# Three more groups of the shared expert behind the last routing step, five instead of eight in the last stage, four outgoing buffers there

## The reference: what is computed

```python
b, s, d = x.shape
T = b * s
xf = x.reshape(T, d)
shared = jax.nn.silu(xf @ Sg) * (xf @ Su) @ Sd          # Sg, Su: 256 x 256, Sd: 256 x 256
probs = jax.nn.softmax(xf @ Wr, axis=-1)                 # 16 experts
topk_p, topk_i = jax.lax.top_k(probs, K)                 # K = 2
...
    y = jax.nn.silu(xf @ wg) * (xf @ wu) @ wd
    return (acc + y * c[:, None], None)
...
return (routed + shared).reshape(b, s, d)
...
x = x + _L1_ffn_ref(_layernorm(x, axis=-1), L1_ffn_Wr, L1_ffn_Wg, L1_ffn_Wu, L1_ffn_Wd, L1_ffn_Sg, L1_ffn_Su, L1_ffn_Sd)
```

## Time and profile before

| | us |
|---|---|
| median of three runs | 1645.22 |
| the profiled execution | 1644.97 |
| its span | 1643.2 |
| PE busy in it | 1487.4 (91%) |
| DVE busy in it | 1018.6 (62%) |
| last instruction of VectorE in `finish` ends | 1640.5 |

### The profile page before, as it was taken

The page is one execution under the profiler, slowest core; times in us unless marked ns, Lnnn a source line. Parts: engine busy times, 40 slices in busy tenths (PEclk is TensorE's granted clock), DMA queues, the critical chain, the costliest instruction groups (busy, mean ns, idle before and its releaser), DMA issues. The chain is left out here.

```text
span 1643.2 us, 31228 instructions
## 1 busy us (share of the span) xinstructions
PE 1487.4 (91%) x9905; PEld 1114.3 (68%) x9905; DVE 1018.6 (62%) x3468; ACT 736.6 (45%) x1544; POOL 572.3 (35%) x994
## 2 busy tenths in 40 slices
PE   5999999983999999699799999999999597589987
PEld 3776676772999999565566666666666386468876
DVE  3345555453444444499898888888886286645558
ACT  3444444430222222345177777777777242244420
POOL 4123333344222222245532332322333165635530
PEclk9999999986999999899899999999999798889999
DMA  7001111115777777668857666667761575745556
GB/s 234 1 26 36 49 46 52 39 58 157 212 212 213 212 212 212 211 229 259 203 75 98 98 90 90 92 89 98 98 89 40 143 240 187 171 129 156 161 159 220
DMA packets 150592, 221.74 MB, mean 135 GB/s; under 512 B 23648, under 2 KB 98144, under 8 KB 150304
## 3 DMA queue, kind: packets, MB, share of 16 engines
q1 hardware_dynamic: 127904, 170.58, 45.2%
q0 software_dynamic: 13344, 36.55, 6.4%
q10 hardware_dynamic: 9184, 12.61, 2.5%
HBM read 141.16 MB, written 78.25 MB: 134 GB/s over the span
## 5 line engine op out<-in xcount | busy, mean ns | idle before, releaser
L2095 ACT ACTIVATE t_probs<-t_ps_st 128x512 f32<-128x512 f32 x576 | 313.2, 597 | 124.9 <-PE t_ps_st L2147 122.4
L2073 DVE CUSTOM_DVE_ANT_0 whole_sum<-t_ps_s,t_later 128x512 bf16<-128x512 f32 (+3 forms) x512 | 285.5, 586 | 14.0 <-PE t_ps_s L2133 11.9
L2049 POOL TENSOR_SCALAR_AFFINE_SELECT t_probs<-t_probs 128x128 f32<-128x128 f32 x512 | 137.4, 300 | 330.5 <-ACT t_probs L2095 328.9
L2133 PE MATMUL t_ps_s<-t_ks,t_qs 96*128 96x512 f32 (+3 forms) x768 | 247.8, 362 | 0.5 <-ACT t_neg_max L2085 0.5
L2147 PE MATMUL t_ps_st<-t_qs,t_ks 128*128 128x512 f32 (+3 forms) x768 | 242.7, 365 | 0.8 <-ACT t_probs L2095 0.8
L2147 PEld LDWEIGHTS t_ps_st<-t_qs,t_ks 128*128 128x128 f32 x768 | 136.8, 189 | 73.6 <-ACT t_probs L2095 40.2
L2073 DVE CUSTOM_DVE_ANT_0 whole_sum<-t_ps_s,t_later,t_first_max 128x512 bf16<-128x512 f32 (+3 forms) x256 | 140.5, 549 | 47.8 <-PE t_ps_s L2133 47.8
L2162 PE MATMUL t_ps_o<-t_probs,t_vs 128*17 128x256 f32 (+1 forms) x2560 | 154.9, 361 | 0.5 <-ACT whole_sum L2102 0.5
L2133 PEld LDWEIGHTS t_ps_s<-t_ks,t_qs 96*128 96x128 f32 x768 | 138.7, 190 | 18.0 <-DVE t_first_max L2073 1.6
L1460 POOL DMA_INDIRECT outputs_dram<-m_y,m_place x71 | 68.1, 959 | 208.8 <-DVE m_place L1535 201.1
L1490 PE MATMUL m_ps_h<-m_xt,m_w_t 128*128 128x128 f32 x1136 | 140.7, 278 | 0.0
(11 more groups left out here) (340 smaller groups left out, 2652.1 us busy)
## 6 DMA issues: line engine op xcount, KB each, us to landing
m_w_t<-in_w_dram SPq DMA_DIRECT2D x71, 512.0 KB, 4.4
t_qs<-qkt_dram SPq DMA_DIRECT2D x128, 128.0 KB, 5.6
t_ks<-qkt_dram SPq DMA_DIRECT2D x128, 128.0 KB, 5.7
m_x_t<-gathered_dram SPq DMA_DIRECT2D x79, 128.5 KB, 2.1
m_x_t<-gathered_dram SPq DMA_DIRECT2D x71, 129.0 KB, 2.1
d_ye<-outputs_dram SPq DMA_DIRECT2D x8, 1024.0 KB, 8.2
qkt_dram<-d_hi ACTq DMA_DIRECT2D x32, 256.0 KB, 5.2
qkt_dram<-d_lo SPq DMA_DIRECT2D x32, 256.0 KB, 7.2
```

Of the source, the lines that this page charges most:

```text
L2049: nc.gpsimd.affine_select(out=diag, in_=diag, compare_op=ALU.is_ge, fill=0.0, base=0, pattern=[[1, P]], channel_multiplier=-1).then_inc(ma ...
L2073: nc.vector.tensor_tensor_reduce(out=seen[:, (NP * p + x) % (RS + 1), 0:keys], in0=bank_of(p, x)[:, 0:keys], in1=masks, scale=1.0, scalar= ...
L2095: nc.scalar.activation(probs[:, p % 2, i // NST, base:base + STC], ps_st[(NX * p + i) % RT][:], ACT.Exp, scale=HD ** -0.5).then_inc(exp_re ...
L2133: nc.tensor.matmul(bank_of(p, x)[:, 0:keys], q[0:MAX_ROW, head, qc * P:(qc + 1) * P], k[0:MAX_ROW, head, k0:k0 + keys], start=True, stop=T ...
```

## The change

`finish` now computes the shared expert of five groups (11 to 15), and `back` that of eleven. The three added ones, groups 8 to 10, don't stand in the pipeline of ticks, which stays as it is, but behind it: on TensorE after the last ranking, on VectorE around the making of the tile list, on ScalarE between the closing writes. They use `k_scaled` in place of `k_sh`, and `k_ps_wo` for the result in place of `k_ps_u`, so that one group's way down does not hold up the next one's way up. ScalarE's two exponentials and its last four closing writes move behind added sigmoids.

In `finish` the 16 groups stand in six slots: one gate, then one or two plain groups, then one shared group. `f_y` has four buffers (Y = 4), the wait for a store stands right before the instruction that writes `f_y`, and the stores are issued by ScalarE, behind the sigmoid of the slot; SyncE issues loads alone.

```diff
-SHARED_BACK = 8
+SHARED_BACK = 11
+EARLY_SHARED = 8
...
+            def late_gate(k):
+                dve.wait_ge(sig_ready, k + 1)
+                nc.vector.tensor_tensor(scaled[:, k % 2], ps_g[:], scaled[:, k % 2], ALU.mult).then_inc(gated, 1)
+                dve.wait_ge(gated, k + 1)
+                dve.wait_ge(u_done, k + 1)
+                nc.vector.tensor_tensor(scaled[:, k % 2], ps_u[:], scaled[:, k % 2], ALU.mult).then_inc(h_ready, 1)
+
+            def late_add(k):
+                dve.wait_ge(y_done, k + 1)
+                these = total[:, k * G:(k + 1) * G]
+                nc.vector.tensor_tensor(these, these, ps_wo[k % 2][:], ALU.add).then_inc(y_added, 1)
...
+            for k in range(EARLY_SHARED, SHARED_BACK):
+                late_sigmoid(k)
+                if k - EARLY_SHARED < 2:
+                    close_regions(act, closed[k - EARLY_SHARED], closed[k - EARLY_SHARED + 1])
             act.wait_ge(shifted_ready, 2)
             nc.scalar.activation(soft[:], soft[:], ACT.Exp).then_inc(exp_ready, 1)
             nc.scalar.activation(soft_best[:], soft_best[:], ACT.Exp).then_inc(exp_ready, 1)
-            close_regions(act, E // 2, E)
...
+            def late_up(k):
+                cols = slice(k * G * P, (k + 1) * G * P)
+                wait(pe, gated, k)
...
+                if k == EARLY_SHARED:
+                    pe.wait_ge(y_added, k)
+                else:
+                    pe.wait_ge(h_ready, k)
...
+            def late_down(k):
+                pe.wait_ge(h_ready, k + 1)
...
-    R = 4
+    R, Y = 4, 4
     ye = sb("f_ye", [P, R, 2, G, DM])
-    y = sb("f_y", [P, 2, G, DM])
+    y = sb("f_y", [P, Y, G, DM])
...
-    order = []
-    for k in range(NS + 1):
-        order += [k] if k < SHARED_BACK else []
-        order += [SHARED_BACK + k - 1] if k else []
+    slots = [[SHARED_BACK * k // (NS + 1) + n for n in range(SHARED_BACK * (k + 1) // (NS + 1) - SHARED_BACK * k // (NS + 1))]
+             for k in range(NS + 1)]
+    for k in range(NS):
+        slots[k + 1].append(SHARED_BACK + k)
+    order = [g for slot in slots for g in slot]
...
-                wait(dve, stored[q % 2], 16 * (q // 2))
+                if not shared:
+                    wait(dve, stored[q % Y], 16 * (q // Y))
...
+                    wait(dve, stored[q % Y], 16 * (q // Y))
+                    nc.vector.tensor_tensor(y[:, q % Y], total[:, g * G:(g + 1) * G, :], ps_y[k % 2][:], ALU.add).then_inc(summed, 1)
...
+            for k in range(NS + 2):
+                if live(k):
+                    sigmoid(k)
+                if k:
+                    for q in range(last_of[k - 2] if k > 1 else 0, last_of[k - 1]):
+                        store(q)
```

More of the change, by code:

```diff
@@ L2286, in going_up @@
     def going_up(tick):
-        return (tick - FIRST_SHARED) // 2 if tick >= FIRST_SHARED and (tick - FIRST_SHARED) % 2 == 0 and tick < FIRST_SHARED + 2 * SHARED_BACK else None
+        return (tick - FIRST_SHARED) // 2 if tick >= FIRST_SHARED and (tick - FIRST_SHARED) % 2 == 0 and tick < FIRST_SHARED + 2 * EARLY_SHARED else None
     def close_regions(eng, first, last):
@@ L2507, in _ @@
                                            op1=ALU.add).then_inc(entry_ready, 1)
+            late_gate(EARLY_SHARED)
             dve.wait_ge(list_done, 1)
             nc.vector.tensor_copy(tile_list[:], ps_list[0:1, :, 0:n_list]).then_inc(list_ready, 1)
+            for k in range(EARLY_SHARED + 1, SHARED_BACK):
+                late_gate(k)
+                late_add(k - 1)
+            late_add(SHARED_BACK - 1)
             dve.wait_ge(list_ready, 2)
@@ L2630, in _ @@
             last.then_inc(list_done, 1)
+            for k in range(EARLY_SHARED + 1, SHARED_BACK):
+                late_up(k)
+                late_down(k - 1)
+            late_down(SHARED_BACK - 1)
 def finish(nc, sb, pb, sem, c, outputs, kept, total, xnt, weights, out_dram):
@@ L2651, in finish @@
     loaded = [sem(f"f_loaded{s}") for s in range(R)]
-    stored = [sem(f"f_stored{s}") for s in range(2)]
+    stored = [sem(f"f_stored{s}") for s in range(Y)]
     NS = NG - SHARED_BACK
-    order = []
-    for k in range(NS + 1):
-        order += [k] if k < SHARED_BACK else []
-        order += [SHARED_BACK + k - 1] if k else []
+    slots = [[SHARED_BACK * k // (NS + 1) + n for n in range(SHARED_BACK * (k + 1) // (NS + 1) - SHARED_BACK * k // (NS + 1))]
[3 more added lines that the diff above has]
+    order = [g for slot in slots for g in slot]
+    last_of = [sum(len(slot) for slot in slots[:k + 1]) for k in range(NS + 1)]
     turn = {g: q for q, g in enumerate(order)}
@@ L2688, in add_up @@
                     dve.wait_ge(one_added, G * q + j + 1)
-                    nc.vector.scalar_tensor_tensor(out=total[:, t, :] if shared else y[:, q % 2, j, :], in0=ye[:, q % R, 1, j, :],
+                    nc.vector.scalar_tensor_tensor(out=total[:, t, :] if shared else y[:, q % Y, j, :], in0=ye[:, q % R, 1, j, :],
                                                    scalar=kept["prob"][:, t, 1:2], in1=total[:, t, :], op0=ALU.mult, op1=ALU.add).then_inc(two_added, 1)
@@ L2699, in _, with sigmoid @@
                     gate(k)
[L2700 to L2703, removed]
+                for g in slots[k]:
+                    add_up(g)
         @block.scalar
         def _(act):
-            for k in range(NS):
+            def sigmoid(k):
                 act.wait_ge(g_done, k + 1)
@@ L2710, in _, with store @@
                 nc.scalar.activation(sig[:, k % 2], ps_g[k % 2][:], ACT.Sigmoid).then_inc(sig_ready, 1)
+            def store(q):
+                g = order[q]
+                act.wait_ge(two_added, G * q + G)
+                if g >= SHARED_BACK:
+                    act.wait_ge(summed, g - SHARED_BACK + 1)
+                act.dma_start(out_dram[g * G * P:(g + 1) * G * P, :].rearrange("(j p) n -> p j n", p=P), y[:, q % Y]).then_inc(stored[q % Y], 16)
+            for k in range(NS + 2):
[4 more added lines that the diff above has]
+                        store(q)
+            for s in range(Y):
+                act.wait_ge(stored[s], 16 * (NG // Y))
         @block.sync
@@ L2718, in load @@
                     sp.dma_start(ye[:, q % R, i], outputs[first:first + G * P, :].rearrange("(j p) n -> p j n", p=P)).then_inc(loaded[q % R], 16)
[L2720 to L2727, removed]
-                load(q)
[L2729 to L2734, removed]
+            for q in range(NG):
+                load(q)
+            sp.wait_ge(two_added, G * NG)
         @block.tensor
```

26 lines of the change are left out of this document (25 added, 1 removed).

## The result

The changed kernel was timed at 1634.8 us, the median of five executions, beside 1645.3 for the kernel before. Four of them took 1628.4 to 1636.0 us; the fifth, at 1657.6, ran at a lower mean granted clock (0.911 against 0.954 to 0.964) and isn't in the ratio. The ratio is 0.9917 (95% interval 0.9899 to 0.9934): about 13.7 us faster. That is a little more than my range held (1632.2 as its lower end, where 0.9917 x 1645.3 is 1631.6). Repeated, the same kernel gave 0.9935 (0.9912 to 0.9957) and 0.9941 (0.9921 to 0.9962), 10.7 and 9.8 us. So the gain is under 1% of the whole, and in all three comparisons clear of no change; how much it is can be read better from the traces, since both kernels scatter: 24 executions of the kernel before, beside the first repeat, lay between 1639.0 and 1650.3.

A forecast was written before the change was run, and what follows sets the result against it. It took `finish` as bound by VectorE and, through two outgoing buffers, by transfers, which would bound it after the change. Span 1643.2 - 1634.1 = 9.1 us less, nothing in `back`: 1645.2 - 9.1 = 1636.1 us, range 1632.2 to 1641.0.

The forecast's parts named there:

- Faster, and where: Whole kernel: span 9.1 us shorter, all of it in `finish`, nothing in `back`.
- The routing end at price 0: End of `back`: nine added blocks at full clock end by 1440.4, before SyncE's wait ends at 1441.2; cost 0.
- The slack of 0.8 us: End of `back`: the added work's last sum ends 0.8 us before SyncE is let go.
- a rival with seven slow blocks: End of `back`: clock falls, seven blocks cost 1.7 us more each, time 1647.2 us; chance 0.05.
- The store waits go: `finish`: with four buffers VectorE's 5.6 us of waits for stores disappear.
- VectorE's path: `finish`: VectorE's gates and sums run from 1596.69 to 1628.2 if no load or store is waited for.
- The front: Start of `finish`: unchanged up to the second gate's end at 1596.69.
- the transfers' term: `finish`: 38.9 us of transfers at 317 GB/s, share 0.96, take 40.5; last load 1629.0, end 1634.1.
- The sign that I had named for the forecast: `finish`: a DMA share of 0.9 or more in the profile after.
- the rival built on it: `finish`: transfers keep ahead and VectorE stays the bound, 1632.9 us; chance 0.20.
- The rule set against the forecast: `finish`: about 358 GB/s per core, so 12.59 MB take 35 us, VectorE bounds, span ends at 1630.9.
- the share as now: `finish`: transfers keep their 0.80 share, last load at 1637.1, time 1644.2 us; chance 0.10.

The follow-up runs named there:

- e1: The changed kernel run again with no edit; median 1632.3 us, ratio 0.9935 to the kernel before.
- e3: The changed kernel with two outgoing buffers and SyncE's stores as before, the three groups still moved; median 1643.5 us, ratio 0.9986 to the kernel before.
- e4: The changed kernel with plain groups 0 and 1 ahead of the first gate of the last stage; ratio 0.9929 to the kernel before.
- e9: The changed kernel again with no edit, on another chip; median 1644.9 us, ratio 0.9941 to the kernel before.
- e11: The changed kernel with ten shared groups in the routing stage instead of eleven; one execution, 212.3 us from the last ranking to the end.
- e2: The kernel before with four outgoing buffers, the late wait and ScalarE's stores, still eight shared groups in the last stage; median 1640.5 us, ratio 0.9972.
- e7: The changed kernel with stores issued by SyncE in one row with the loads, four buffers kept; one execution, last stage 48.2 us.
- e5: The changed kernel without the first of each group's two sums in the last stage, same bytes; 42.0 us from first load's issue to end, against 45.5.
- e6: The changed kernel loading only the first expert's result per group and adding it twice; 44.4 us from first load's issue to end, against 45.5.

## Why the prediction was right or wrong

- **Faster, and where**: right. The last stage gave 10.5 us of the first profile's 10.1; I had 9.1. `m1` changed by 0.4.
- **The routing end at price 0**: right in the first profile. The last sum ended 18.0 us behind the last ranking, where I had 18.1, and the closing writes, though issued later, did not hold up the block. The slack of 0.8 us was rightly seen as narrow. That the added blocks start at the full clock was right in the first profile, e1, e3 and e4; on the two later chips the first one ran at the low clock, which the prediction had only as a rival with seven slow blocks, at 0.05. One slow block fitted in, the two of e9 cost 1.3 us. That any missed pause would bring the low level back was too strong, as the 0.90 us of e11 show.
- **The store waits go**: right, and by the four buffers, as argued (e2: 5.0 us of the last stage, I had 5.6). ScalarE's queue has no part in it (e7).
- **VectorE's path**: right. From the end of the second gate I had 31.5 us; measured are 31.8, of which 0.29 for a load. The front was off by 1.9 us: the stage began 0.4 us later, and the rest is the longer low clock. There the sentence that TensorE isn't waited for even at the low clock was wrong, VectorE waited 1.74 and 0.48 us for it.
- **The step that failed** is the transfers' term: "That is 317 GB/s when every engine works", and with it the last load at 1629.0 and the bound. I divided the bytes by the busy share and took the quotient for a capacity. It isn't one: the quotient rose with the load, from 316 GB/s in the middle of the stage before (253 / 0.80) to 352 in e5 (384 / 1.09), and the share has no ceiling at 0.96 or at 1, as the 1.06 of the earlier trace rows had already shown. e5 moved 381 to 384 GB/s for 15 us at a share of 1.09, and e6 showed that bytes don't set the stage. Instead of 3 to 4 us of waits for loads VectorE had 0.29. The sign that I had named for the forecast, a share of 0.9 or more, appeared all the same (0.94 from 1596 to 1628) and proved nothing. The single microsecond of 370 GB/s in the earlier trace rows was the better guide, and the rival built on it came true: VectorE stays the bound. I gave it 0.20. Its own reason, that the transfers gain by not sharing a queue with the stores, did not show: in e7 they share it, and VectorE waits for nothing but TensorE. It forecast a span of 1630.9; the front (1.9) and the load (0.3) make up the 1633.1 of the profile.
- **The rule set against the forecast**: the Trainium skill's page "DMA: Bandwidth & Descriptors" (Where 436 GB/s comes from) led to the right outcome. The rate here went above its 358 GB/s for HBM to SBUF: 384 with loads and stores mixed. That isn't against the page, which in its section on measured bandwidth gives about 358 for each core when both cores of a pair stream, and 425 GB/s for one core alone; this program runs on one core. My estimate took the lower figure.
- **The size**: the timed ratio is beyond the range by 0.6 us; both repeats lie within it. Of the 13.7 us, 10.6 are shown in the changed blocks. The rest could be chance in the untouched part, which is argued from its scatter and not shown. The median of all five, 1634.8 us, lies between my 1636.1 and the rival's 1632.9; that is luck, since the waits that I forecast did not occur.
- **A slip in the chances**: the share as now (0.10) and half of the clock's case come to 0.125, not 0.11. Nothing hangs on it.

## What to carry to other kernels

A busy share below 1 with some GB/s beside it doesn't give the capacity by division; look for the fullest single windows, or take away the other engine's work and read the rate. Best of all, take away bytes and see whether the time moves. When a stage waits for stores through two buffers, moving work out of it and adding buffers are one change: alone they gave 2.0 and 5.0 us of the last stage, together 10.5. Work hidden behind a fixed wait should be priced at the low clock for its first blocks, since the slack is spent by whichever execution starts cold.

## What the runs showed that I had not expected

- The length of the low clock at a stage's start varies: one or two blocks of 8 passes (3.50 and 1.89 us before, 3.75 and 3.19 after) behind the same pause of 4.96 us. It cost VectorE 1.3 us more of waiting. Over all fourteen profiles the second block of the last stage took 1.89 us in four and 2.3 to 3.2 in ten.
- Code that no edit touched took 1422 to 1423 us until the last ranking in the first pair, 1424 to 1429 on the chip of e1 to e4, and 1428 to 1432 on the two others. There some 3.6 us of it are the pause ahead of the last ranking; why it occurs stays open, and the kernel before was not profiled on those chips.
- 384 GB/s of 1 KB packets, with loads from one queue and stores from another, held for 15 us.
